# Moving the rows of a second layer norm from VectorE to ScalarE in the token stages of a two-layer transformer

## What is computed

```
x = x + attention0(layernorm(x), ctx)      # softmax((q @ k.T * tau + delta) / sqrt(32)) @ v, then Wo
x = x + experts0(layernorm(x))             # gate logits = layernorm(x) @ gate.T, top 8 of 32
x = x + attention1(layernorm(x), ctx)
x = x + light(rms_norm(x)) + heavy(rms_norm(x[chosen]))
# layernorm(v) = (v - mean(v)) / sqrt(var(v) + 1e-5), over the row, without scale or shift
```

## Time and profile before

| | |
|---|---|
| median of 3 runs | 3379.52 us (3376.65 to 3384.28) |
| profiled execution | 3375.24 us, its span 3373.5 us |
| PE busy | 3187.6 us (94%), 17270 matmuls |
| DVE busy | 2720.3 us (81%) |
| ACT busy | 1560.8 us (46%) |
| POOL busy | 2097.0 us (62%) |
| granted TensorE clock, mean | 0.98 |

### The profile page before, as it was taken

The page is one execution under the profiler, slowest core; times in us unless marked ns, Lnnn a source line. Parts: engine busy times, 40 slices in busy tenths (PEclk is TensorE's granted clock), DMA queues, the critical chain, the costliest instruction groups (busy, mean ns, idle before and its releaser), DMA issues. The chain is left out here.

```text
span 3373.5 us, 55546 instructions
## 1 busy us (share of the span) xinstructions
PE 3187.6 (94%) x17270; PEld 2498.1 (74%) x17270; DVE 2720.3 (81%) x5412; ACT 1560.8 (46%) x5463; POOL 2097.0 (62%) x2416
## 2 busy tenths in 40 slices
PE   7999999999979999999999699999999969999998
PEld 5677777777647888888888567777777758778886
DVE  4788888889746888888887389999999879967775
ACT  1766666676621111111111377777777745321111
POOL 1766766667635777777777477777777753433333
PEclk8999999999989999999999899999999989999999
DMA  7345454454465666766676444555554457730111
GB/s 219 100 137 169 119 172 134 141 155 134 136 210 131 167 176 165 179 168 166 166 179 155 111 128 135 159 164 144 150 171 136 138 166 287 274 102 13 26 13 25
DMA packets 285026, 491.01 MB, mean 146 GB/s; under 512 B 54258, under 2 KB 75058, under 8 KB 284018
## 3 DMA queue, kind: packets, MB, share of 16 engines
q1 hardware_dynamic: 252146, 409.92, 39.3%
q0 software_dynamic: 32256, 77.65, 12.3%
q10 hardware_dynamic: 384, 0.52, 0.1%
HBM read 250.32 MB, written 136.96 MB: 115 GB/s over the span
## 5 line engine op out<-in xcount | busy, mean ns | idle before, releaser
L984 ACT ACTIVATE c_pr<-ps,t_negmax 128x154 f32<-128x154 f32 x1024 | 384.8, 392 | 197.3 <-DVE t_negmax L731 196.3
L731 DVE TENSOR_REDUCE t_negmax<-ps 128x4 f32<-128x616 f32 x512 | 404.1, 789 | 53.2 <-PE ps L1053 52.7
L984 ACT ACTIVATE t_pr<-ps,t_negmax 128x154 f32<-128x154 f32 x1024 | 384.8, 392 | 107.9 <-DVE t_negmax L731 103.0
L754 DVE COPY t_pTm<-ps 128x512 f32<-128x512 f32 x448 | 306.2, 683 | 118.6 <-PE ps L1066 114.5
L649 POOL TENSOR_TENSOR t_pr<-t_pr,t_inv 128x512 f32<-128x512 f32 x256 | 274.8, 1073 | 191.0 <-DVE t_inv L746 189.9
L649 POOL TENSOR_TENSOR c_pr<-c_pr,t_inv 128x512 f32<-128x512 f32 x256 | 271.7, 1061 | 195.2 <-DVE t_inv L746 193.9
L1053 PE MATMUL ps<-t_kst,t_stack 98*128 98x154 f32 x2048 | 352.8, 291 | 26.7 <-DMA t_stack<-t_q_low 10.0
L1053 PEld LDWEIGHTS ps<-t_kst,t_stack 98*128 98x128 f32 x2048 | 279.5, 193 | 39.1 <-issue 18.3
L81 PE MATMUL ps<-e_xT_high,e_wgu_high 128*128 128x512 f32 x768 | 301.6, 393 | 1.4 <-DVE e_xT_low L1639 1.4
L83 PE MATMUL ps<-e_xT_high,e_wgu_low 128*128 128x512 f32 x768 | 299.3, 390 | 0.0
L82 PE MATMUL ps<-e_xT_low,e_wgu_high 128*128 128x512 f32 x768 | 299.0, 389 | 0.0
(11 more groups left out here) (359 smaller groups left out, 9313.8 us busy)
## 6 DMA issues: line engine op xcount, KB each, us to landing
t_stack<-t_q_high SPq DMA_DIRECT2D x1016, 64.0 KB, 2.0
c_wgu_in<-in_gate_upT SPq DMA_DIRECT2D x32, 1536.0 KB, 6.4
t_stack<-t_q_low SPq DMA_DIRECT2D x512, 64.0 KB, 2.0
x_dram<-c_wide_rows SPq DMA_DIRECT2D x32, 1024.0 KB, 7.6
c_wd_in<-in_downT SPq DMA_DIRECT2D x32, 768.0 KB, 11.5
t_xbo<-in_x SPq DMA_DIRECT2D x16, 1024.0 KB, 5.7
xw_dram<-t_z SPq DMA_DIRECT2D x16, 1024.0 KB, 5.3
t_xbo<-x_dram SPq DMA_DIRECT2D x16, 1024.0 KB, 11.2
```

The source lines that it names most:

```text
L731: dve.tensor_reduce(negmax[:, u, :], flat[:, at:at + HG * APART].rearrange("p (h n) -> p h n", h=HG)[:, :, 0:KEYS], AX, ALU.max, negate=Tr ...
L754: dve.tensor_copy(pTm[:, g % 2, :, t * P:(t + 1) * P], ps[:, 4, :].rearrange("p (h n) -> p h n", h=HG)).then_inc(s["pTm"], 1)
L984: op = act.activation(pr[:, u % 4, h, :], flat[:, col:col + KEYS], ACT.Exp, bias=negmax[:, u, h:h + 1], accum_out=total[:, u, h:h + 1])
```

## The change

The rows of `z` are made by ACT, as `Identity(xs * rstd + shift)` with a scale and a bias per row, in place of DVE. POOL makes the bias, `shift = -mean * rstd`, with two more 128 x 4 instructions and their waits behind `rstd`. Since ACT reads `xs` later than DVE did, POOL's `rstd_of` and DVE's first residual of a group now also wait for the rows of the group before. The four rows stand at four slots, and the turns of `z`, their copies and the first square are moved by one or two slots.

```
-        Z = (3, 5, 8, 22)
+        Z = (4, 6, 9, 22)
-        ZD = (4, 11)
+        ZD = (5, 11)
-        NZ = (0, 0, 1, 1) if gate else (3, 7, 10, 13)
+        NZ = (0, 1, 2, 3) if gate else (1, 4, 8, 10)
-        ZA = (5, 24)
+        ZA = (7, 24)
-        SQ = (8, 13, 14, 22)
+        SQ = (9, 13, 14, 22)
...
                 pool.wait_ge(s[kind + "_mv"], TG * n + TG)
+                if kind == "s":
+                    reached(pool, s["z" if gate else "xl"], TG * n)
...
+                if kind == "s":
+                    pool.tensor_scalar(shift[:], mv[:, which, :, 0], -1.0, None, ALU.mult).then_inc(s["s_minus"], 1)
+                    pool.wait_ge(s["s_minus"], n + 1)
+                    pool.wait_ge(s["s_rstd"], n + 1)
+                    pool.tensor_tensor(shift[:], shift[:], rstd[:, which, :], ALU.mult).then_inc(s["s_shift"], 1)
...
                 if t == 0:
                     reached(dve, s["x_stored"], 16 * j)
+                    reached(dve, s["z" if gate else "xl"], TG * j)
...
-                        for t in range(TG):
-                            if at == NZ[t]:
-                                normed(1, "s", j, xs, z_of(j), "z" if gate else "xl", (t,))
...
+            def side_rows(j, t):
+                act.wait_ge(s["s_shift"], j + 1)
+                if t == 0 and (gate or j < NG - 1):
+                    reached(act, s["z_stored"], 16 * j)
+                if t == 0 and gate:
+                    reached(act, s["z_mm"], DC * j)
+                act.activation(z_of(j)[:, t, 0:D], xs[:, t, :], ACT.Identity, bias=shift[:, t:t + 1],
+                               scale=rstd[:, 1, t:t + 1]).then_inc(s["z" if gate else "xl"], 1)
...
+                    if at in NZ and prev2:
+                        side_rows(j, NZ.index(at))
```

More of the change, by code:

```diff
@@ L321, in token_phase @@
         ve, rstd = sb("ve", [P, 2, TG]), sb("rstd", [P, 2, TG])
-        half, eps, tick = (sb(n, [P, TG]) for n in ("half", "eps", "tick"))
+        half, eps, tick, shift = (sb(n, [P, TG]) for n in ("half", "eps", "tick", "shift"))
         z = sb("z", [P, TG, D if gate else XS])
@@ L340, in token_phase @@
                  "q_mm q_out q_high q_low scored negmax shared exped inv normed p_mm pTm pTt pv oT_high oT_out proj resid "
-                 "s_stats s_mv s_ve s_rstd xl z z_mm zT_dve zT_act side_mm top "
+                 "s_stats s_mv s_ve s_rstd s_minus s_shift xl z z_mm zT_dve zT_act side_mm top "
                  "others shifted shared_out picked stepped carried chosen summed inverted weighted w_stored "
```

## The result

The changed kernel takes 3447.28 us (median of 4 runs, 3443.5 to 3450.0) against 3381.9 us for the kernel before (4 runs): ratio 1.019, 95% interval 1.0166 to 1.0214, 1.9% slower. The profiled execution took 3443.5 us, its span 3441.8 us: 68.3 us more than that of before. PE was busy 3213.8 us (93%), DVE 2641.1 (77%, 79 us less), ACT 1646.8 (48%, 86 us more), POOL 2094.5 (61%); mean granted clock 0.973.

What follows compares the result with a forecast made beforehand. PE was taken as the bound, so a lighter DVE is worth only PE's waits for it. 44 - 10 + 2.5 + 0 + 2.3 + 11 = 50 us on 3375.24 gives 3425, plus 4.3 for a median: 3429 us, range 3400 to 3452.

Steps and rivals of the forecast that it cites:

- the forecast's own case: Whole kernel: PE waits for the rows and the clock falls in some turns, 3429 us, 1.5% slower; chance 0.55.
- rival 2: First stage: the clock falls in every turn, perhaps for longer, +61 or more, 3441 to 3455 us; chance 0.13.
- the credit: First stage, slot 11: lighter DVE is early, so PE's wait for its copy goes, 0.7 us a turn, -10 us.
- the clock: First stage, behind the new wait: half clock loses some 1.6 us a fall; half of 22 us taken, +11.
- The wait at slots 2 to 4: First stage: PE's turn of `z` waits for ACT's rows, 3.2 us longer in 14 full turns, +44 us.
- The last two turns: First stage's last two turns, without exponentials: +1.1 for the last, +1 to +2 for the one before, together +2.5.
- The second stage: Second token stage's turns: PE's waits are not reached by lightening DVE, 0 us; bounds -20 and +8.
- Rival 3: Faster, 3355 us: DVE really holds the exponentials, so second-stage waits go, -20, and about -5 in the first; chance 0.07.
- Its end: Second stage's end: ACT makes four rows and four squares in series, so POOL's power starts later, +2.3 us.
- The rows' price: ACT: each new row costs 0.62 us in its list, 2.5 us of a turn.
- POOL's two instructions: POOL, ahead of a unit's scaling: two small instructions, 0.45 us with the hand-over, taken as costing nothing.
- DVE's busy time: Sign of being right: DVE's busy time falls by about 100 us without any gain.

Runs made afterwards that it cites:

- e4: Changed kernel with sixteen dummy transposes of the identity on PE ahead of its wait for the rows: 3431.19 us, 1.0145 of the kernel before.
- e7: Kernel before, rows still on DVE, with only the turns of `z` and their copies at the new slots: 3385.49 us, 1.0019.
- e5: Changed kernel with first-stage rows early (slots 0, 0, 1, 1) and the turns of `z` and their copies at their old slots: 3376.19 us, 0.9993.
- e6: Changed kernel with the turn of `z` one slot further, behind the first half of `query` n = 3: 3400.94 us, 1.0064 of the kernel before.
- e12: Kernel before, rows on DVE, with only the first stage's two `mark` instructions moved from slot 9 to 8: 3368.48 us, 0.9963.
- e1: Changed kernel with the change in the first token stage only, the second as in the kernel before: 3449.45 us, 1.0201.

## Why the prediction came out as it did

The forecast was 3429 us, slower; it is 3447, slower and inside the range. But the forecast's own case, a clock that falls in half of the turns, is not what happened: rival 2 is (a fall in every turn, 3441 to 3455), to which it gave 0.13. The direction and the wait were foreseen for the right reason; that the sum comes within 18 us is in part luck, since two terms of some 10 us (the credit and the clock) were wrong the same way and only the width of the range held them. Two of its bounds do not come out of its own terms: the upper end is 3450 and not 3452 (3379.5 with 44, 2.5, 2.3 and 22), and the two waits of the earlier trace rows are 12.6 us, some 14 for the stage, and not 17. Neither bears on the outcome.

- **The wait at slots 2 to 4, +44.** Right. Foreseen 3.2 us, 14 times. The one turn shown gives 3.24, and e4's turn grew by 3.14. What it left out is how it divides: 1.0 us is a wait for exponentials and 2.0 for the row. Part of the first (0.3 us, e7) comes from the slots and not from the rows.
- **The credit, -10.** Wrong; this is the step that failed in its reasoning. "DVE is early at slot 11" did not hold: the wait is 0.6 or 0.7 us in the changed kernel and in e5 alike. DVE's lead ends where it next waits for PE, at slot 9, and the wait at slot 11 is made behind that, by `mark` and a cast beside POOL. The prediction had used this very argument for the second stage (no row between the last slot where DVE had caught up and the wait) and did not put it to the first.
- **The clock, +11.** The price of a fall was right: 1.6 us foreseen, 1.57 measured. The number was not: 13 falls and not seven, some 20 us, so that the turn came to 58.03 us, past the 56 or 57 named as a sign of being right. The earlier trace rows had PE busy 1.56 of 3.4 us ahead of a fall, and the new wait left it 0.96 of 3.5. A wait that stands at the same place of every turn speaks for a fall each time or never (e6, with shorter waits, has none) rather than for "half".
- **The last two turns, +2.5.** Too small. Their logits start 32.06 and 12.59 us after the ones ahead of them, before 27.76 and 11.38: +4.3 and +1.2, 5.5 us. In the turn before the last PE stood 1.92 us at the turn of `z` (991.79), though there are no exponentials: row 2 stood behind the attention output, for whose product ACT had waited 5.67 us, and the copy of probabilities and row 3 followed. The clock fell there once more too (6.8 us from 992.1).
- **The second stage, 0.** Right within 4 us. The waits that it named did not change, but the steady turns gained 0.31 us each, 4.0 us over 13 spacings, through waits of PE for DVE too short for the earlier trace rows; "that is all a lighter DVE could ever give back" left them out. Rival 3 (relief of DVE frees ACT and so PE, 20 us faster) falls: ACT's wait for maxima did go from 82.4 to 37.5 us, and PE's waits for ACT stayed.
- **Its end, +2.3.** Right: from the start of the first row to the start of the power 6.06 us (2814.79 to 2820.85) against 4.37 before (2746.04 to 2750.41), +1.7, and 0.5 for POOL's two instructions ahead of the row (2814.24 to 2814.79). The last two powers lie 11.12 us apart and 8.93 before, +2.2.
- **The rows' price, 0.62 us in a series.** 0.71 measured, 0.1 us on each of two rows in the path. It is inside the 3.24.
- **POOL's two instructions, 0.** Right: 232 and 202 ns, and no wait of PE for POOL that was not there.
- **DVE's busy time, about 100 us less (a sign of being right).** It fell by 79. The rows' own durations sum to 113 us, but the cast of the queries now meets POOL more often, 103.9 us over the program in place of 94.9, and DVE's instructions overlap each other less.

Put together by what was measured: 14 full turns lost 3.4 (the first) and 59.9 us (the other 13), 63.3, which is 14 waits of 3.24 and 13 falls of 1.57 (65.8) less 2.5 that stays unexplained; the last two lost 5.5. That is the 68.9 us of the logits.

## What to carry to other kernels

A piece that leaves a full engine for a half idle one keeps its place in line, and the place decides: the same ScalarE rows cost 65 us at four slots and nothing at the two earlier ones (with the turn of `z` in its old slots), since ScalarE's free time lay ahead of the product it had to wait for and not behind it. Before giving credit for a lighter engine, walk its list from the wait back to the last point where it had caught up; what lies between the two counted most here, and moving 1 us out of there (11 us in e12) was worth more than taking 3 us a turn away in front of it (2 to 3 us in e5, within noise). A wait of TensorE of this kind can have two prices, its own length and the half clock behind it: in the changed kernel both came in each of 13 turns, and in e6, with shorter waits, only the first. Where such a wait can't be removed, work put into it can pay even if nobody needs that work (16 us in e4).

## What was not expected of the hardware

- The clock fell 13 times, each 58.03 us behind the last, without a miss, and 13 times again in e1 (one of them for 6.8 us). What makes it that regular was not tried.
- Sixteen transposes of the identity in 1.92 us kept the clock at 1.00 where 0.96 busy of 3.5 us did not; a wait of 1.0 us together with one of 0.5 (e6) cost no fall either.
- A 128x512 cast on DVE took 0.40 us alone, 0.91 when it started 0.42 us behind a POOL instruction of 1.04 us, and 1.51 when it started 0.11 us behind one of 1.34 us: beside POOL it ended 0.28 or 0.29 us behind POOL's end in both. Moving another instruction by one slot changed the 1.51 to 0.91.
